# A fused attention and mixture-of-experts layer: the first part (normalise, project, spread) in another order

## What is computed

```
xn  = layernorm(x)
qkv = xn @ Wqkv.T + b          # 16 query heads of 16, one key head, one value head
attention, causal, 16 heads against the shared key and value; out projection + bias
logits = xn @ w_router.T       # 16 experts, softmax, the best 4, weights normed to 1
ffn = sum over the chosen experts of coeff * (silu(xn @ gate) * (xn @ up)) @ down
out = x + attention + ffn
```

## Time and profile before

| | |
|---|---|
| median of 3 runs | 425.07 us (424.75 to 428.62) |
| the profiled execution | 425.48 us, its span 423.6 us |
| busy: PE, PEld | 381.6 us (90%), 300.7 us (71%) |
| busy: DVE, ACT, POOL | 232.7 us (55%), 216.8 us (51%), 301.2 us (71%) |
| DMA | 57.48 MB, 136 GB/s on average |

### The profile page before, as it was taken

The page is one execution under the profiler, slowest core; times in us unless marked ns, Lnnn a source line. Parts: engine busy times, 40 slices in busy tenths (PEclk is TensorE's granted clock), DMA queues, the critical chain, the costliest instruction groups (busy, mean ns, idle before and its releaser), DMA issues.

```text
span 423.6 us, 7998 instructions
## 1 busy us (share of the span) xinstructions
PE 381.6 (90%) x2505; PEld 300.7 (71%) x2505; DVE 232.7 (55%) x588; ACT 216.8 (51%) x361; POOL 301.2 (71%) x327
## 2 busy tenths in 40 slices
PE   3999879999999999999999999999999999999800
PEld 2343644555555454799999999999999999999700
DVE  5778889998897861343444444444444344444300
ACT  3586134557766677654554554554454455455200
POOL 7999311249997276777788888888878887888820
PEclk9999989999999999999999999999999999999955
DMA  7789996899687799954545454455454555556045
GB/s 225 244 210 236 223 199 131 189 184 201 165 191 115 246 284 317 285 141 66 75 74 76 78 78 78 66 79 77 78 78 70 77 84 75 76 73 80 4 81 118
DMA packets 54201, 57.48 MB, mean 136 GB/s; under 512 B 11456, under 2 KB 49008, under 8 KB 53904
## 3 DMA queue, kind: packets, MB, share of 16 engines
q0 software_dynamic: 15440, 21.51, 30.7%
q1 hardware_dynamic: 25760, 22.83, 23.2%
q10 hardware_dynamic: 12960, 12.62, 11.3%
HBM read 37.40 MB, written 23.33 MB: 143 GB/s over the span
## 4 chain that ended last, share of the span: by engine, by line
PE 70%; DVE 12%; issue 5%; ACT 3%; DMA 3%; POOL 2%; POOLq 0%; ACTq 0%; SPq 0%; DVEq 0%
PE bank L815 31%; PE bank L824 15%; DVE pmax L1214 6%; PE bank L761 4%; PE bank L692 4%; PE bank L806 4%; PE bank L750 3%; PE bank L713 2%; PE bank L788 2%; DVE wgu L1331 1%; DMA qs_late<-nm 1%; PE bank L782 1%; PE bank L668 1%; PE bank L773 1%; POOL out_dram L625 1%
## 5 line engine op out<-in xcount | busy, mean ns | idle before, releaser
L1419 DVE COPY late<-bank 128x256 f32<-128x256 f32 x79 | 33.5, 425 | 106.3 <-PE bank L806 106.3
L824 PE MATMUL bank<-wdn,late 128*128 x316 | 81.4, 380 | 0.2 <-DVE late L1423 0.2
L815 PEld LDWEIGHTS bank<-late,choice 128*128 128x128 f32 x640 | 77.5, 192 | 4.0 <-issue 1.8
L1012 ACT ACTIVATE pt<-bank 128x512 f32<-128x512 f32 x96 | 55.8, 598 | 46.9 <-PE bank L750 45.9
L815 PE MATMUL bank<-late,choice 128*128 128x128 f32 x640 | 78.0, 275 | 1.0 <-ACT choice L1090 1.0
L815 PEld LDWEIGHTS bank<-late 128*128 128x128 f32 x624 | 75.6, 192 | 2.4 <-issue 0.3
L1095 ACT ACTIVATE late<-bank 128x256 f32<-128x256 f32 x79 | 30.3, 384 | 89.6 <-PE bank L815 89.6
L815 PE MATMUL bank<-late 128*128 128x128 f32 x624 | 76.0, 275 | 0.1
L625 POOL DMA_INDIRECT out_dram<-pt,slots x40 | 62.9, 1573 | 13.5 <-issue 11.3
L1214 DVE TRANSPOSE_TENSOR_REDUCE pmax<-bank 128x16 f32<-128x512 f32 x96 | 65.4, 701 | 10.7 <-PE bank L692 10.0
L625 POOL DMA_INDIRECT odd_d<-pt,slots x39 | 61.3, 1572 | 12.5 <-issue 9.8
(11 more groups left out here) (158 smaller groups left out, 495.8 us busy)
## 6 DMA issues: line engine op xcount, KB each, us to landing
qs_late<-q_d SPq DMA_DIRECT2D x40, 128.0 KB, 5.2
q_d<-early SPq DMA_DIRECT2D x16, 256.0 KB, 4.9
wgu<-in_L_ffn_w_gate_dram ACTq DMA_DIRECT2D x8, 512.0 KB, 8.2
wgu<-in_L_ffn_w_up_dram ACTq DMA_DIRECT2D x8, 512.0 KB, 10.1
wdn<-in_L_ffn_w_down_dram ACTq DMA_DIRECT2D x8, 512.0 KB
qs_wgu<-q_d SPq DMA_DIRECT2D x24, 128.0 KB, 5.8
xs<-in_L_attn_x_dram SPq DMA_DIRECT2D x4, 512.0 KB, 4.1
xn_d<-early SPq DMA_DIRECT2D x4, 512.0 KB, 4.0
```

What stands on the lines that cost most here:

```text
L815: mm = pe.matmul(bank[:, 2 + j % 2, f * P:(f + 1) * P], wst[j % 2][:, c, f * P:(f + 1) * P], xT[:, j % 2, c, :], start=(c == 0), stop=(c = ...
L824: mm = pe.matmul(bank[:, 4 + j % 2, 0:D], hT[:, j % 2, c, :], wdn[:, bass.ds(e * FC + c, 1), :], start=(c == 0), stop=(c == FC - 1))
L1012: act.activation(pt[:, G % 2, n % NU, :], bank[:, 3 + N % 2, :], ACT.Exp).then_inc(exp_done, 1)
L1419: dve.tensor_copy(xT[:, j % 2].rearrange("p c t -> p (c t)"), bank[:, 0, 0:D]).then_inc(xgT_ready, 1)
```

## The change

- PE's order in a group becomes: queries (`project_q`), then values, logits and keys (`project_rest`), then the transposes of the next group. The 12 maximum blocks of batch 0 stand between the matmuls of groups 2 and 3, six in each, all on two banks.
- On ACT the query roundings come first in each group (`split_q`), the normalisation of group 1 is cut in pieces between them, and the copy of the query weights comes before `normalise(0)`.
- DVE's order is written out: the leftovers of the queries, then of the keys, and the row maxima in pairs between them.
- Keys no longer go through DRAM: `spread_k` copies them from SBUF to SBUF with four DMAs per group. A query load is two DMAs of 32 partitions in place of four of 16. One zero fill of `odd_d` (1 MB) moves from before the first group's stores to behind the first part.
- The first half of the choice moves from DVE's group 2 into batch 0, and the rest of the choice, the counting and the row lists move later (LIST_AT by 4 steps).
- PE runs 14, 7 and 4 dummy matmuls ahead of the first projection.

```diff
@@ PE
             pe.wait_ge(masks, 4)
+            stay_busy(14)
             pe.wait_ge(w_in, 16 * N_W)
...
-                if N == NU + 2:
+                if N == NB + 2:
                     pe.wait_ge(vr_ready, NG)
                     pe.wait_ge(kl_ready, NG)
...
+            def project_q(g):
                 pe.wait_ge(xT_act, g + 1)
                 pe.wait_ge(xT_dve, g + 1)
+                for m in range(KC):
+                    if g:
+                        pe.wait_ge(ql_ready, KC * (g - 1) + m + 1)
...
+                    mm.then_inc(proj_ps, 1)
+                    if g >= 2:
+                        first = 6 * (g - 2) + 2 * m
+                        scores_for_max(0, first)
+                        scores_for_max(0, first + 1)
+
+            def project_rest(g):
                 if g:
                     pe.wait_ge(vr_ready, g)
                     pe.wait_ge(kl_ready, g)
...
                 mm.then_inc(proj_ps, 1)
+                if g >= 2:
+                    scores_for_max(0, 6 * (g - 2) + 4)
+                    scores_for_max(0, 6 * (g - 2) + 5)
+            stay_busy(7)
             transpose_x(0)
+            stay_busy(4)
             pe.wait_ge(w_act, 2)
             for g in range(NG):
-                project(g)
+                project_q(g)
+                project_rest(g)
+                if g + 1 < NG:
+                    transpose_x(g + 1)
@@ ACT
             for g in range(NG):
+                if g >= QBUF:
+                    act.wait_ge(q_stored[g - QBUF], 64)
+                split_q(g, 0)
+                if g == 0:
+                    normalise(1, 2, 3)
+                split_q(g, 1)
+                if g == 0:
+                    normalise(1, 3, 4)
+                act.wait_ge(proj_ps, 3 * g + 3)
...
                 if g < NG - 1:
                     keep_xT(g + 1)
                 if g + 2 < NG:
                     root(g + 2)
...
                 if g + 2 < NG:
                     normalise(g + 2)
@@ DVE
+            for g in range(2):
+                keep_ql(g, 0)
+                keep_ql(g, 1)
+                keep_kl(g)
+                keep_xT(g + 1)
+                scale(g + 2)
                 if g == 0:
                     measure(3)
+            keep_ql(2, 0)
+            row_max(0, 0)
+            row_max(0, 1)
+            keep_ql(2, 1)
+            row_max(0, 2)
+            row_max(0, 3)
+            keep_kl(2)
+            keep_xT(3)
+            row_max(0, 4)
+            row_max(0, 5)
+            keep_ql(3, 0)
+            row_max(0, 6)
+            row_max(0, 7)
+            keep_ql(3, 1)
+            row_max(0, 8)
+            row_max(0, 9)
+            keep_kl(3)
+            row_max(0, 10)
+            row_max(0, 11)
@@ SP
+            def spread_k(g):
+                sp.wait_ge(kl_ready, g + 1)
                 for r in range(4):
+                    sp.dma_start(k_all[16 * r:16 * r + 16, g * GW:(g + 1) * GW].bitcast(F32),
+                                 khl[:, g % 2, r // 2, :].bitcast(F32)).then_inc(k_spread[g], 16)
...
+            store_xn(0)
+            for g in range(NG):
+                store_q(g)
+                if g + 1 < NG:
+                    store_xn(g + 1)
+                spread_k(g)
                 if g < 3:
                     if g == 0 or g == 2:
                         sp.wait_ge(q_stored[g // 2], 64)
...
             sp.wait_ge(nm_ready, 1)
             load_q(2, 1)
-            load_k(2 * GW, T)
+            zero_odd(0)
@@ POOL
+            copy_k(0)
+            pool.wait_ge(k_ready, 2)
             from_rows(1)
             pool.wait_ge(qs_padded, 16)
...
+            copy_k(1)
+            copy_k(2)
...
             from_rows(2)
             pool.wait_ge(qs_padded, 24)
+            for g in range(NG):
+                add_bias(g)
```

More of the change, by code:

```diff
@@ L648, in _, with stay_busy @@
         def _(pe):
+            def stay_busy(n):
+                for _ in range(n):
+                    pe.matmul(bank[:, 4, 0:P], ident[:, :], ident[:, :], start=True, stop=True)
             pe.wait_ge(masks, 4)
+            stay_busy(14)
             pe.wait_ge(w_in, 16 * N_W)
@@ L878, in count_choices @@
                 mm.then_inc(place_ps, 1)
[L880 to L889 removed]
+            pe.wait_ge(ql_ready, KC * NG)
             for n in range(MAX_AHEAD - NB):
                 scores_for_max(1, n)
[L892 removed]
+                stay_busy(1)
                 if n == 1:
@@ L932, in normalise @@
                     act.wait_ge(xn_stored[g % 2], 16 * (g // 2))
-                for u in range(GT):
+                for u in range(first, last):
                     t = g * GT + u
@@ L1215, in row_max, with keep_ql, keep_kl @@
                                   apply_transpose=True).then_inc(max_done, 1)
-            for g in range(NG):
+            def keep_ql(g, m):
+                dve.wait_ge(qh_ready, KC * g + m + 1)
+                dve.scalar_tensor_tensor(out=qhl[:, g % QBUF, 1, m, :], in0=bank[:, 3 + m, :],
+                                         scalar=bq_s[:, m:m + 1], in1=qhl[:, g % QBUF, 0, m, :].bitcast(F32),
+                                         op0=ALU.add, op1=ALU.subtract).then_inc(ql_ready, 1)
+            def keep_kl(g):
                 dve.wait_ge(kh_ready, g + 1)
```

192 lines of the change are left out of this document (64 added, 128 removed).

## The result

The changed kernel takes 437.8 us (median of 4 runs, 435.26 to 441.04) against 426.64 us (4 runs, 424.75 to 428.62): ratio 1.0265, 95% interval 1.0174 to 1.0356. It is slower, as forecast, but by 11.2 us and not by 4.5, and outside the range (425.3 to 433).

A forecast was written before the change was run, and what follows sets the result against it. PE was taken to bound the experts and nearly fill the first part, DVE batches 0 and 1. First part 3.8 + choice 0.7 = +4.5 on the profiled 425.48, 430.0; median forecast 429.6 us, 8-in-10 range 425.3 to 433.

The forecast's parts named there:

- At nothing: Effects priced at zero: POOL's later lists, the moved zero fill, earlier keys, query loads, the exponential's table load.
- The first part: Before the batches: split of the first maximum at 54.55 instead of 50.74, 3.8 us later, bounds 3.5 and 4.3.
- The start: First projection: starts at 13.5 instead of 11.79, bounds 13.2 and 14.0, at full clock from there.
- the turns: Group to group in the first part: one group takes 8.3 us, before 7.9; group 1 at 21.8, group 2 at 30.2.
- the gap of group 2: First part: PE waits from about 34.0 for row maxima, idle 2 to 3 us; group 3 starts at 42.7.
- the rival of the falling clock: Clock falls in group 2's gap: L701 takes 1.7 us more, parts of group 3 a little; +2.4, 432.0; chance 0.17.
- The choice: Batches 0 and 1: its moved half costs DVE 2.7 us, mostly absorbed by idle time; priced 0.7, bounds 0 and 2.7.
- Contention: `scale(3)` on DVE in group 2: takes 2.5 us if it meets POOL, about 1.4 if not; 2.5 taken.
- keys and query loads: Keys arrive with 6 us to spare; batch 0's queries are thin, 0 to 1 us; both taken at 0.
- The dummies: Before the first projection: 14 dummies on PE lift the clock, so the first queries run at full clock.

The follow-up runs named there:

- a_lists_early: Changed kernel with counting, slots and row lists as early as its choice allows; 448.21 us against 442.88, ratio 1.0161.
- a_keys_first: Changed kernel with POOL's copy of the keys of batch 5 behind 12 one-hot tables instead of 20; 438.8 us, ratio 1.0266.
- a_fill_gap: Changed kernel with 12 dummy matmuls on PE after the second query half of group 2; 440.35 us, ratio 1.0285.
- a_norm_behind: Changed kernel with ACT's normalisation of group 3 behind the second query split of group 2; 451.49 us against 441.58, ratio 1.0238.
- b_dma: Kernel before with only the change's DMA part: keys spread from SBUF to SBUF, query loads of 32 partitions; 441.71 us, ratio 0.998.
- a_mended3: a_mended2 with POOL's bias additions of groups 0 and 1 where the change has them, groups 2 and 3 behind the split; 443.95 us, ratio 1.008.
- a_mended: Changed kernel with lists early, half the choice before batch 0, transposes between queries and values, group 3's normalisation behind query roundings; 447.19 us against 441.58, ratio 1.0139.
- a_turn: Changed kernel with the next group's transposes on PE between queries and values/keys; 456.9 us against 442.88, ratio 1.0304.
- a_bias_late: a_norm_behind with POOL's 16 additions of the output bias held until the maxima are split; 436.37 us against 427.12, ratio 1.0214.
- a_mended2: a_bias_late with the lists early and the choice of the first two groups ahead of group 2's splits; 432.04 us against 427.12, ratio 1.0111.

## Why the prediction was wrong

**The failed step** is a sentence under "At nothing": "POOL's lists end four steps later; it waits 10.1 us before its gathers". I looked for slack at the end of POOL's queue and not for what stands inside it. Between the tables stands the copy of the keys of batch 5, whose slack before was about 1 us, and PE waits for it. In the profile it cost 7.0 us of the 15.6; alone on the kernel before it costs 5.5. The trace of before held the price: four steps of batch 2 are 4 x 14.6 / 12 = 4.9 us, less 0.9 of slack 4.0, which turns my +4.5 into +8.5, and the fallen clock comes on top. PE's wait was 4.7 us.

**The first part** was right in its mechanism as the profiled execution shows it, and the term was too small there, 5.75 for 3.8; the other executions of the same first part lost 3.3 and 4.4 us against the profile before, on both sides of the forecast. The start, the turns and the gap of group 2 came to within about 0.3 us up to the first row maximum. Part of that is luck: a_lists_early starts 1.3 us earlier with the same first part. Behind it the rival of the falling clock held in this execution: L706 took 1.3 us more, group 3 started 1.9 late, group 3 itself took 0.6 more (44.58 to 57.06, 12.5 for 11.85), and the way from the split to the first block gave 0.6 back (5.54 for 6.1). My reason against this rival, that matmuls of 0.43 fill the time around the gap, was no reason. But the gap is not what makes the clock fall in general: in a_keys_first and a_lists_early, which alter nothing here, it fell already at the first query matmuls of group 2, behind the turn's pause of 1.64 us (3.64 us instead of 1.95), as it did in a_fill_gap and a_norm_behind (3.08 and 3.65).

**The choice** was mis-sized: 0.7 for 2.3. The row said that DVE was busy 27.3 of the 30.1 us of batches 0 and 1, 91%; the idle rest, in pieces between dependent maxima, did not take in the work. I should have taken the bound of 2.7, not the one near 0. Against the kernel before, the whole loss of batches 0 and 1 was 2.7 us in the profiled execution and 1.1 in a_keys_first, the same code up to there; what gave part of the 2.3 back, no run prices.

**Contention** was right for `scale(3)` (2.7 for 2.5). The trace agrees with the rule cited for the steps with two inputs (0.52 and 0.60 us); but L1142, with one input, also took 0.54 instead of 0.17, which the rule as I cited it does not cover. One reading of mine was wrong: POOL was beside the fast call of line 1141 too (0.161 us at 7.10), but with an instruction that only writes (L490, IOTA, 7.05 to 7.26); that agrees with the rule as well. That contention would matter at the joins, which I had in none of my terms, only the experiments showed; in the profiled execution of the changed kernel it cost nothing, as the join missed the train by 1.1 us.

**At nothing, and rightly so:** keys and query loads (b_dma, 0.998). The dummies, too, did to the first queries what the forecast said (3.67 us, and 6.61 without them). That a_mended3, where stall, choice and gap are mended, loses 0.8%, 3.5 us, and so comes near the forecast of +4.5, is luck: the forecast had a gap and a share of the choice in it.

**Open:** in every kernel with this first part but a_mended the clock falls at least once between 22 and 42 us, wherever the gap is, and in every one again somewhere between 52 and 86 us, from the last maxima of the first part to the end of batch 1. I could not name what sets the place, and executions of the same code differ in it. The 3.2 us between the profiled execution and the median are of that size: a_keys_first, the same code up to batch 2, had block 24 2.9 us earlier (92.21 for 95.15), with the clock at 0.94 in batches 0 and 1 where the profiled execution had 0.78 and 0.90.

## What to carry to other kernels

When a step is moved, list every instruction behind it in the queue of each engine that it feeds, and give each its own due time: slack at the end of a queue says nothing about what stands in its middle. A full busy share does not say what waits: POOL was as full in batch 3 before as after. Where an engine's own work sets the pace of a stretch, as DVE's did here, price work that is added there at its full length. After removing a gap look at the granted clock and at what now runs side by side: here another pair of instructions met, and one of them took 2.22 us instead of 0.23. And before a gain of 1 or 2 us is read from one profile, look how far two executions of the same code lie apart.

## What the runs showed of the hardware

A DVE operation with both inputs in SBUF, 128x64 and 0.23 us long, took up to 3.69 us beside POOL's back-to-back additions (each 0.72 us, also two inputs in SBUF). In six of the seven kernels in which additions made a join longer it ended 0.08 to 0.09 us behind the last addition; in four of these (a_turn, a_norm_behind, a_bias_late, a_mended2) it had missed one to five changes from one addition to the next. The Trainium skill, "SBUF — State Buffer", "Who interferes with whom", says that such a pair contends for a shared port; the trace agrees. That the price is always the rest of the train does not follow. In a_mended the join waited only for the running addition, and so did two steps of `scale(3)` in the kernel before, each ending 0.02 us behind the addition beside it, while further additions followed:

```profile
25.97 2.78 POOL L517 TENSOR_TENSOR xs<-xs,bo 128x256 f32<-128x256 f32 x4
27.44 0.65 DVE L1141 TENSOR_TENSOR rstd<-rstd,std 128x4 f32<-128x4 f32 x1
```

The rest of the train is the upper bound; the runs do not show what decides.

The same program took 3.8% longer on some chips (442.88 for 426.64 us). From the start of the last score block to the end of the span it was 268 us (a_norm_behind) against 255.8 before and 256.3 in a_bias_late; and batch 6 (blocks 72 to 84) took 12.2 to 16.4 us on these chips and 11.4 to 11.9 on the others. So most of the difference lies in the experts and the rest in the last batches. I have no run that tells why.
